# Row-maxima mask in four quarters of the array, routing in 18 steps, transposed maxima copied by ScalarE

## The chip, the cores and the metric

The kernel runs on one core of a Trainium2 chip. The metric is the device time of one execution in microseconds (us). An iteration below is one pass of the attention loop, in which one sequence of 512 rows goes through; there are 16 sequences.

## The reference, cut to what matters

```python
# x: (16, 512, 128); 16 heads of 8; 8 experts, hidden width 512; float32
x = _layernorm(x + attention(x))            # causal softmax attention
# mixture of experts on xn, which is x normalized once more, with gamma and beta
probs = softmax(xn @ Wg.T)                  # 8 experts
top1 = argmax(probs); top2 = argmax(probs without top1)
t1v, t2v = probs[top1], probs[top2]
gates = [t1v, t2v] / (t1v + t2v + 1e-9)
out = sum over the two of gate * (gelu(xn @ W1[e] + b1[e]) @ W2[e] + b2[e])
x = _layernorm(x + out)
```

With `best` the largest logit and d the second largest minus best, the gates are 1/z and exp(d)/z, z = 1 + exp(d) + 1e-9 * sum(exp(logit - best)).

## The kernel before, in words

Attention and routing run in one software pipeline, `iterations`: in iteration i the kernel computes the scores and values of sequence i, the row maxima of sequence i (second half) and of sequence i+1 (first half), the output projection of i-1, the gating input of i-2 and the routing of i-2 and i-3. An iteration has 16 steps h. The order of each engine is written out by hand, as a function `body` for each. The expert stage (lines 1129 to 1145) and the last normalization follow; neither is touched by the diff.

The maxima of a sequence are taken in 24 units (`maxima`, line 1011). In a unit TensorE multiplies queries by keys into one of three slots of `ring` (line 1037: stationary 64 rows by 128 columns, once for each half of the array's rows, so that two heads run beside each other), adds the causal mask by a product of a diagonal and `pastb` in bfloat16 (line 1052: four products a unit), and VectorE reduces the slot (`maximum`, line 1189). 16 of the 24 units mask one block of 128 columns in each head, 8 mask two. The scores (`scores`, line 1006) use the slots in turn with them: unit n of the scores waits for the maximum of unit n-2 to be taken, unit n of the maxima for the exponentials of scores unit n-1. The scores, the products of queries and keys and the mask all use the array as two tiles of 64 rows by 128 columns; the small products of line 973 and the projections (899, 904, 910, 934, 965) and transposes (888) use it whole, the values (1069) and the transposes of the maxima (917) in tiles of 128 by 32.

The maxima of a group of four heads and their rounding rest (`split_max`) are transposed by TensorE into `ps_m` (`st_mT`, line 917, at h = 1, 5, 9, 13), copied to `mt` (`copy_max`, line 1218, VectorE, right after the first maximum of that step) and placed beside the queries by a DMA on ScalarE's queue (`place_max`, at h = 2, 6, 10, 14). `ps_m` is used by one thing after another in the order of `MISC`: after mT come kT (h = 2, line 899), uT (h = 6 and 14) and nT (h = 10), and each waits for `freed` of the one before.

Routing is a list of 20 steps (`ROUTING`, line 1258), one or two small VectorE operations each, with a semaphore between one step and the next. Steps 0 to 5 of sequence i-2 stand at half-steps 26 to 31 of an iteration, 6 to 11 of i-3 at half-steps 0 to 5, the rest at 9 to 16. Lines 1283 to 1287 (steps 15 to 19) make the gates, at half-steps 12 to 16: half-step 14 is h = 7. In h = 6 and later GpSimd masks probabilities (line 598), writes rows by indirect DMA (line 610) and multiplies by gamma (line 664, h = 7).

## Time and profile before

| | |
|---|---|
| median of 3 runs | 1107.22 us (1107.21 to 1108.87) |
| profiled execution, its own time | 1104.55 us |
| its span | 1102.5 us |
| PE busy | 959.9 us, 87% |
| DVE (VectorE) busy | 816.1 us, 74% |
| ACT (ScalarE) busy | 665.9 us, 60% |
| POOL (GpSimd) busy | 637.5 us, 58% |
| granted TensorE clock, mean | 0.971 |
| chain that ended last | PE 50%, DVE 20%, issue 10%, DMA 6%, POOL 6% |

The busy shares are means over the whole span. The pipeline of attention and routing fills about two thirds of it, and the expert stage the rest. The chain that ended last is followed back from the last instruction, at each step to what released it. Ends of PE's products are modelled; their starts are what to compare.

### The profile page before, as it was taken

What the parts mean: (1) busy time and instruction counts of PE and PEld (TensorE: products, weight loads), DVE (VectorE), ACT (ScalarE), POOL (GpSimd) and SP (SyncE); (2) the same over time, 40 slices, a digit from 0 to 9 for tenths busy, and PEclk for the clock granted to TensorE, in tenths of its full rate; (3) what the DMA queues carried; (4) which work ended last, traced back from release to release, by engine and by line L of the source; (5) the groups of instructions that cost most, each with busy time, mean ns of one, the idle gap of its engine ahead of it and who ended that gap; (6) DMA issues with size and microseconds to landing.
All of it is one profiled execution on the core that took longest, in us unless ns stands there. A gap on an engine that the chain in (4) does not pass through costs nothing.

```text
span 1102.5 us, 29583 instructions
## 1 busy us (share of the span) xinstructions
PE 959.9 (87%) x9185; PEld 635.4 (58%) x9185; DVE 816.1 (74%) x2134; ACT 665.9 (60%) x1338; POOL 637.5 (58%) x951
## 2 busy tenths in 40 slices
PE   3789999999999999999999999869899889998750
PEld 1344454454545545545544455339899879998740
DVE  3777879888888888898898888954454464467744
ACT  1256566676666676666666766636566745556552
POOL 7022434754855756657647557547757556557874
PEclk9899999999999999999999999979999999999985
DMA  7523133243243242332432423343322222265515
GB/s 163 191 79 114 52 105 113 60 139 104 65 129 105 86 123 83 114 118 71 125 116 54 137 92 90 104 144 78 86 69 85 74 74 78 72 215 171 170 50 171
DMA packets 134567, 117.74 MB, mean 107 GB/s; under 512 B 56218, under 2 KB 99777, under 8 KB 134240
## 3 DMA queue, kind: packets, MB, share of 16 engines
q1 hardware_dynamic: 121808, 96.37, 30.0%
q0 software_dynamic: 8704, 17.06, 4.6%
q10 hardware_dynamic: 3904, 2.43, 1.0%
q8 instruction: 78, 1.28, 0.5%
q14 instruction: 73, 0.60, 0.2%
HBM read 65.26 MB, written 53.81 MB: 108 GB/s over the span
## 4 chain that ended last, share of the span: by engine, by line
PE 50%; DVE 20%; issue 10%; DMA 6%; POOL 6%; ACT 3%; SPq 3%; ACTq 1%; DVEq 0%; POOLq 0%
PE ring L1145 9%; PE ring L1129 9%; DVE negmax L1189 9%; PE ps_v L1069 7%; PE ring L1006 6%; PE ring L1037 5%; PE ring L1052 3%; SPq L397 2%; POOL y_d L633 2%; PE ps_m L899 2%; PE ps_m L917 2%; DVE rv L1285 2%; PE ps_m L934 2%; PE ps_m L904 1%; DVE mt L1218 1%
## 5 line engine op out<-in xcount | busy, mean ns | idle before, releaser
L728 ACT ACTIVATE probs<-ring 128x768 f32<-128x768 f32 (+1 forms) x384 | 337.5, 882 | 211.9 <-PE ring L1006 208.3
L1189 DVE TENSOR_REDUCE negmax<-ring 128x2 f32<-128x1024 f32 (+3 forms) x512 | 410.6, 815 | 62.7 <-PE ring L1052 56.3
L598 POOL TENSOR_SCALAR_AFFINE_SELECT probs<-probs 128x512 f32<-128x512 f32 x256 | 163.1, 639 | 287.0 <-ACT probs L728 285.4
L837 ACT ACTIVATE vpad<-ring,b_s 128x128 f32<-128x128 f32 x576 | 164.3, 369 | 104.9 <-PE ring L1129 103.7
L633 POOL DMA_INDIRECT y_d<-vpad,xs x144 | 146.6, 1018 | 109.9 <-DVE vpad L1488 80.5
L1006 PE MATMUL ring<-qarea,kside 64*128 64x512 f32 (+3 forms) x1024 | 177.7, 385 | 28.6 <-DVE negmax L1189 20.0
L1006 PEld LDWEIGHTS ring<-qarea,kside 64*128 64x128 f32 x1024 | 86.6, 185 | 183.1 <-issue 119.4
L1069 PE MATMUL ps_v<-probs,vpad 128*32 128x512 f32 (+3 forms) x2048 | 180.7, 449 | 4.0 <-POOL probs L598 4.0
L1037 PE MATMUL ring<-kside,qarea 64*128 64x256 f32 (+2 forms) x1024 | 165.0, 360 | 17.3 <-DMA qarea<-qk_d 10.4
L1145 PE MATMUL ring<-qarea,vpad 128*128 x1152 | 158.6, 281 | 18.3 <-ACT vpad L837 17.8
L1129 PE MATMUL ring<-vpad,w_t 128*128 128x128 f32 x1152 | 156.2, 279 | 8.9 <-issue 8.5
L1145 PEld LDWEIGHTS ring<-qarea,vpad 128*128 128x128 f32 x1152 | 140.6, 192 | 26.6 <-issue 23.9
L1129 PEld LDWEIGHTS ring<-vpad,w_t 128*128 128x128 f32 x1152 | 141.2, 193 | 13.3 <-issue 12.9
L610 POOL DMA_INDIRECT rows_d<-xn,slot x128 | 128.8, 1006 | 25.9 <-issue 24.4
L1052 PE MATMUL ring<-pastb,diagb 64*128 64x128 bf16 (+1 forms) x1536 | 125.4, 242 | 0.0
L1037 PEld LDWEIGHTS ring<-kside,qarea 64*128 64x128 f32 x1024 | 88.3, 189 | 30.6 <-issue 10.5
L1472 DVE COPY w_t<-kside 128x512 f32 x144 | 64.6, 449 | 54.1 <-PE ring L1129 42.2
L1488 DVE TENSOR_TENSOR vpad<-ring,xin 128x128 f32<-128x128 f32 x144 | 42.0, 291 | 83.1 <-PE ring L1145 77.9
L1052 PEld LDWEIGHTS ring<-pastb,diagb 64*128 64x128 bf16 x1536 | 45.1, 96 | 54.9 <-issue 39.9
L1069 PEld LDWEIGHTS ps_v<-probs,vpad 128*32 128x32 f32 x2048 | 44.9, 109 | 47.4 <-issue 36.3
L852 ACT ACTIVATE probs<-probs,zrs 128x128 f32<-128x128 f32 x64 | 27.5, 488 | 42.8 <-POOL zrs L697 42.8
L1515 DVE SCALAR_TENSOR_TENSOR probs<-probs,gates 128x128 f32<-128x128 f32 x128 | 35.9, 343 | 11.3 <-DMA probs<-x_d 11.2
(178 smaller groups left out, 1092.5 us busy)
## 6 DMA issues: line engine op xcount, KB each, us to landing
qk_d<-qarea SPq DMA_DIRECT2D x62, 256.0 KB, 2.5
kside<-qk_d SPq DMA_DIRECT2D x96, 128.0 KB, 3.0
qarea<-qk_d SPq DMA_DIRECT2D x90, 128.0 KB
xs<-rows_d SPq DMA_DIRECT2D x144, 66.0 KB, 1.9
probs<-y_d SPq DMA_DIRECT2D x16, 512.0 KB, 4.5
xin<-L_attn_x SPq DMA_DIRECT2D x16, 256.0 KB, 2.9
att_d<-attt SPq DMA_DIRECT2D x128, 32.0 KB
rows<-att_d SPq DMA_DIRECT2D x16, 256.0 KB
```

The lines of the kernel that those rows point to most:

```text
L598: pool.affine_select(out=diag, in_=diag, pattern=[[0, 4], [1, P]], compare_op=ALU.is_ge, fill=0.0, base=0, channel_multiplier=-1).then_inc ...
L610: pool.indirect_dma_start(rows_d, bass.IndirectOffsetOnAxis(ap=slot[:, late.parity, k, q:q + 1], axis=0), xn[:, late.parity, q, k, :], Non ...
L633: pool.indirect_dma_start(y_d, bass.IndirectOffsetOnAxis(ap=xs[:, n % RING, D:D + 1].bitcast(I32), axis=0), ys[:, n % RING, :], None, boun ...
L728: nc.scalar.activation(of_unit(h // 2, part), ring[:, 2 * part % 3, :, (0, P, P)[part]:S], ACT.Exp, scale=SCALE).then_inc(sem("exp_done"), 1)
L837: ins = nc.scalar.activation(ht[:, n % 4, c, :], ps_a[:, n % 4, c * P:(c + 1) * P], ACT.Gelu_apprx_tanh, bias=b1_s[:, bass.ds(e, 1), c:c + ...
L1006: ins = pe.matmul(ring[:, 2 * n % 3, half, c0:c0 + S - q0], kside[rows, i.parity, e, g, kb * P:(kb + 1) * P], qside[i.parity][rows, g, q0: ...
L1037: pe.matmul(ring[:, (2 * n + 1) % 3, half, c0:c0 + nk], qside[b.parity][rows, g, qb * P:(qb + 1) * P], kside[rows, b.parity, e, g, 0:nk], ...
L1052: ins = pe.matmul(to, diagb[rows, at:at + P], past, start=False, stop=(c == 1))
L1069: ins = pe.matmul(ps_v[32 * j:32 * j + 32, kb * P:S], vpad[:, b.parity, kb, h, :], of_block(h, kb), start=(g % 2 == 0 and kb == 0), stop=( ...
L1129: ins = pe.matmul(ps_a[:, n % 4, c * P:(c + 1) * P], w1_t[:, n % 2, c * P:(c + 1) * P], xst[:, n % 4, :], start=True, stop=True)
L1145: ins = pe.matmul(ps_s[:, n % 2, 0:D], ht[:, n % 4, c, :], w2_s[:, bass.ds(e, 1), c, :].rearrange("p a d -> p (a d)"), start=(c == 0), sto ...
L1189: ins = nc.vector.tensor_reduce(negmax[:, n // 6 % 2, qb, s:s + 2], ring[:, (2 * n + 1) % 3, :, c0:c0 + nk], AX.X, ALU.max, negate=True)
```

## The change

The mask of a unit is made by four products of 64 by 64 instead of four of 64 by 128: queries 0 to 63 of a block against its 128 keys, queries 64 to 127 against its last 64 keys only, each for both row halves. So the product is written to 64 partitions at a time, and the second pair streams 64 columns for 128 (in the 8 units with two blocks 256 and 128 columns, where it was 256 twice). Routing has 18 steps: the first equality is folded into the multiplication by the table, the difference to the second logit comes out of the reduction itself, and z is one reduction over ten terms, for which ScalarE's exponential has a bias of log(1e-9) and a term of 1 is set once. `copy_max` moves from VectorE to ScalarE, where it stands at the end of h = 1, 5, 9, 13.

```diff
-    ROUTE = 20
+    ROUTE = 18
-        diagb = sb("diagb", [P, 3 * P // 2], BF16)
+        diagb = sb("diagb", [P, P // 2], BF16)
+        terms = sb("terms", [P, QB, E + 2])
+        tiny = sb("tiny", [P, 1])
...
+            pool.memset(terms[:], 1.0)
+            pool.memset(tiny[:], math.log(1e-9))
...
+                        if u == 2 and h % 4 == 1:
+                            copy_max(act, *((i, 1), (i, 2), (i, 3), (nxt, 0))[h // 4])
...
+            def copy_max(act, b, g):
+                if not b.exists(NB):
+                    return
+                need(act, ready("mT"), 4, b, g + 1)
+                need(act, sem("max_placed"), 64, b, 16 * g)
+                nc.scalar.activation(mt[:], ps_m[0:2 * GH, :], ACT.Copy).then_inc(freed("mT"), 1)
...
-                        nc.scalar.activation(rt[:, 2], rt[:, 1], ACT.Exp).then_inc(sem("gate_exp"), 1)
+                        nc.scalar.activation(terms[:, :, 0:E], rt[:, 1], ACT.Exp, bias=tiny[:, :]).then_inc(
+                            sem("gate_exp"), 1)
-                    need(act, sem("route"), ROUTE, i.plus(-3), 8)
-                    nc.scalar.activation(rv[:, 4], rv[:, 3], ACT.Exp).then_inc(sem("gate_exp"), 1)
+                    need(act, sem("route"), ROUTE, i.plus(-3), 7)
+                    nc.scalar.activation(terms[:, :, E], rv[:, 3], ACT.Exp).then_inc(sem("gate_exp"), 1)
...
                 for c in range(2):
-                    at = HALF * (1 - c)
+                    queries = slice(HALF * c, HALF * (c + 1))
                     for half in range(2):
                         rows = half_of(half)
-                        to = ring[:, (2 * n + 1) % 3, half, :]
-                        past = pastb[rows, at:at + P]
+                        to = ring[queries, (2 * n + 1) % 3, half, :]
+                        past = pastb[rows, HALF:(3 - c) * HALF]
                         if n % 3 == 2:
-                            to = to.rearrange("p (a n) -> p a n", n=P)[:, 0:QB:QB - 1, :]
-                            past = past.unsqueeze(1).broadcast_to([HALF, 2, P])
+                            to = to.rearrange("p (a n) -> p a n", n=P)[:, 0:QB:QB - 1, c * HALF:P]
+                            past = past.unsqueeze(1).broadcast_to([HALF, 2, P - c * HALF])
                         else:
                             c1 = (QB - 1 - n % 3) * P
-                            to = to[:, c1:c1 + P]
-                        ins = pe.matmul(to, diagb[rows, at:at + P], past, start=False, stop=(c == 1))
+                            to = to[:, c1 + c * HALF:c1 + P]
+                        ins = pe.matmul(to, diagb[rows, :], past, start=False, stop=True)
...
-                lambda b: [V.tensor_tensor(eq1, lg[:], along(best, E), ALU.is_equal),
-                           V.tensor_tensor(diff, lg[:], along(best, E), ALU.subtract)],
-                lambda b: [V.tensor_tensor(w1c, eq1, wtab[:], ALU.mult)],
+                lambda b: [V.tensor_tensor(diff, lg[:], along(best, E), ALU.subtract)],
+                lambda b: [V.scalar_tensor_tensor(out=w1c, in0=diff, scalar=0.0, in1=wtab[:], op0=ALU.is_equal,
+                                                  op1=ALU.mult)],
...
-                lambda b: [V.tensor_reduce(v2, rest, AX.X, ALU.max)],
-                lambda b: [V.tensor_tensor(eq2, rest, along(v2, E), ALU.is_equal),
-                           V.tensor_tensor(d_best, v2, best, ALU.subtract)],
+                lambda b: [V.tensor_reduce(d_best, rest, AX.X, ALU.max)],
+                lambda b: [V.tensor_tensor(eq2, rest, along(d_best, E), ALU.is_equal)],
...
-                lambda b: [V.tensor_reduce(z, ex, AX.X, ALU.add)],
-                lambda b: [V.scalar_tensor_tensor(out=z, in0=z, scalar=1e-9, in1=e2, op0=ALU.mult, op1=ALU.add)],
-                lambda b: [V.tensor_scalar(z, z, 1.0, None, ALU.add)],
+                lambda b: [V.tensor_reduce(z, terms[:, :, :], AX.X, ALU.add)],
                 lambda b: [V.reciprocal(g(b, 0), z)],
                 lambda b: [V.tensor_tensor(g(b, 1), e2, g(b, 0), ALU.mult)],
...
-                        if h % 4 == 1 and not half:
-                            copy_max(gb, gg)
-                        if 12 <= at < 17:
+                        if 12 <= at < 15:
                             route(late, 3 + at)
```

VectorE's `copy_max` (line 1212) is gone. The product of line 1287 now stands at half-step 14, where the addition of line 1285 stood, and the reciprocal at half-step 13.

## Rows read from the trace of the kernel before

**Rows 1.** Windows: us, busy us and count per engine, TensorE clock, DMA share, GB/s.

```profile
44.40:728.20 683.80, 638.37 (x6533) 339.17 (x6533) 591.70 (x1294) 451.34 (x656) 383.70 (x584) 0.99 0.34 101
```

**Rows 2.** Line 1006: duration ns minimum/median/maximum, first and last start, us.

```profile
L1006 PE MATMUL ring<-qarea,kside x1024: 217/415/792, 44.4 to 728.2; 64*128 64x512 f32 x43, 64*128 64x128 f32 x43, 64*128 64x256 f32 x43, 64*128 64x384 f32 x42
```

**Rows 3.** Waits: engine, line, releaser; us in total, times, longest us.

```profile
PEld ring L1006 <- DVE negmax L1189: 50.9, 91, 1.1
...
PEld ps_m L899 <- DVE mt L1218: 5.6, 9, 0.7
```

**Rows 4.** Groups by line and form: busy us, mean ns; then idle us, releaser.

```profile
L1218 DVE COPY mt<-ps_m 8x512 f32<-8x512 f32 x64 | 42.8, 668 | 0.7 <-PE ps_m L917 0.7
...
L1285 DVE TENSOR_SCALAR rv<-rv 128x4 f32<-128x4 f32 x16 | 24.5, 1531 | 0.0
...
L1284 DVE SCALAR_TENSOR_TENSOR rv<-rv 128x4 f32<-128x4 f32 x16 | 4.0, 248 | 0.0
...
L1272 DVE TENSOR_TENSOR rv<-rv 128x4 f32<-128x4 f32 x16 | 6.7, 421 | 0.0
...
L1286 DVE RECIPROCAL gates<-rv 128x4 f32<-128x4 f32 x16 | 2.6, 163 | 0.0
...
L806 ACT ACTIVATE xnt<-ps_m 128x512 f32<-128x512 f32 x16 | 9.6, 600 | 1.0 <-PE ps_m L888 1.0
```

**Rows 5.** Timeline, PE alone: start us, us, engine, line, operation, tiles.

```profile
347.32 0.50 PE L1006 MATMUL ring<-qarea,kside 64*128 64x512 f32 x2
...
347.65 0.40 PE L1037 MATMUL ring<-kside,qarea 64*128 64x512 f32 x2
...
347.89 0.28 PE L1052 MATMUL ring<-pastb,diagb 64*128 64x128 bf16 x4
...
348.11 1.12 PE L899 MATMUL ps_m<-xt,wk_s 128*128 128x512 f32 x2
...
351.19 0.39 PE L1052 MATMUL ring<-pastb,diagb 64*128 64x256 bf16 x4
...
351.51 1.12 PE L904 MATMUL ps_m<-xt,wq_s 128*128 128x512 f32 x2
...
355.23 0.45 PE L1006 MATMUL ring<-qarea,kside 64*128 64x384 f32 x2
...
355.61 0.19 PE L973 MATMUL ring<-onehot,lowerb 128*128 128x40 bf16 x1
...
356.11 0.28 PE L1052 MATMUL ring<-pastb,diagb 64*128 64x128 bf16 x4
...
356.20 0.42 PE L1006 MATMUL ring<-qarea,kside 64*128 64x256 f32 x4
```

**Rows 6.** Timeline around the routing step of line 1285, one iteration.

```profile
448.14 1.11 POOL L610 DMA_INDIRECT rows_d<-xn,slot  x1 [0.17 <-issue]
...
449.22 1.97 DVE L1285 TENSOR_SCALAR rv<-rv 128x4 f32<-128x4 f32 x1
...
449.27 0.65 POOL L598 TENSOR_SCALAR_AFFINE_SELECT probs<-probs 128x512 f32<-128x512 f32 x1
...
449.87 1.29 POOL L664 TENSOR_TENSOR xc<-xc,gam_b 128x512 f32<-128x512 f32 x1
...
450.77 0.29 PE L1052 MATMUL ring<-pastb,diagb 64*128 64x128 bf16 x4
...
451.58 0.44 PE L1006 MATMUL ring<-qarea,kside 64*128 64x384 f32 x2 [0.52 <-DVE negmax L1189]
...
451.64 1.22 DVE L1189 TENSOR_REDUCE negmax<-ring 128x2 f32<-128x1024 f32 x1
...
452.91 0.44 PE L1006 MATMUL ring<-qarea,kside 64*128 64x256 f32 x4 [0.46 <-DVE negmax L1189]
```

**Rows 7.** Timeline, a two-input DVE operation beside a GpSimd DMA.

```profile
376.02 0.97 POOL L610 DMA_INDIRECT rows_d<-xn,slot  x1 [0.17 <-issue]
...
376.14 0.18 DVE L1209 TENSOR_TENSOR mhl<-negmax,mhl 128x16 fp32r<-128x16 f32 x1
```

More of the change, by code:

```diff
@@ L16 @@
 from contextlib import ExitStack
+import math
 import concourse.bass as bass
@@ L555, in _ @@
             link(pool.memset(lowerb[:], 0.0))
-            mid = diagb[:, HALF:2 * HALF]
-            link(pool.affine_select(out=mid, in_=mid, pattern=[[-1, HALF]], compare_op=ALU.not_equal, fill=1.0,
+            link(pool.affine_select(out=diagb[:], in_=diagb[:], pattern=[[-1, HALF]], compare_op=ALU.not_equal, fill=1.0,
                                     base=0, channel_multiplier=1))
-            pool.affine_select(out=mid, in_=mid, pattern=[[-1, HALF]], compare_op=ALU.not_equal, fill=1.0,
+            pool.affine_select(out=diagb[:], in_=diagb[:], pattern=[[-1, HALF]], compare_op=ALU.not_equal, fill=1.0,
                                base=-HALF, channel_multiplier=1)
@@ L1210, in split_max @@
                                             mhl_of(0).bitcast(F32), ALU.subtract).then_inc(sem("max_split"), 1)
-            def copy_max(b, g):
-                if not b.exists(NB):
-                    return
-                need(dve, ready("mT"), 4, b, g + 1)
-                need(dve, sem("max_placed"), 64, b, 16 * g)
-                nc.vector.tensor_copy(mt[:], ps_m[0:2 * GH, :]).then_inc(freed("mT"), 1)
             def low_part(b, side, name, high, stage):
@@ L1251, in _ @@
             V = nc.vector
-            best, d_best, z, e2, c1, v2, c2 = (rv[:, k] for k in (0, 3, 6, 4, 1, 2, 5))
-            eq1, diff, ex, w1c, m1, rest, eq2, w2c, m2, place, p1, p2 = (rt[:, k] for k in range(12))
+            best, d_best, z, c1, c2 = (rv[:, k] for k in (0, 3, 6, 1, 5))
+            diff, w1c, m1, rest, eq2, w2c, m2, place, p1, p2 = (rt[:, k] for k in (1, 3, 4, 5, 6, 7, 8, 9, 10, 11))
+            e2 = terms[:, :, E]
             def g(b, k):
@@ L1259, in _ @@
                 lambda b: [V.tensor_reduce(best, lg[:], AX.X, ALU.max)],
-                lambda b: [V.tensor_tensor(eq1, lg[:], along(best, E), ALU.is_equal),
-                           V.tensor_tensor(diff, lg[:], along(best, E), ALU.subtract)],
-                lambda b: [V.tensor_tensor(w1c, eq1, wtab[:], ALU.mult)],
+                lambda b: [V.tensor_tensor(diff, lg[:], along(best, E), ALU.subtract)],
+                lambda b: [V.scalar_tensor_tensor(out=w1c, in0=diff, scalar=0.0, in1=wtab[:], op0=ALU.is_equal,
+                                                  op1=ALU.mult)],
                 lambda b: [V.tensor_reduce(c1, w1c, AX.X, ALU.max)],
                 lambda b: [V.tensor_tensor(m1, wtab[:], along(c1, E), ALU.is_equal)],
-                lambda b: [V.scalar_tensor_tensor(out=rest, in0=m1, scalar=NEG, in1=lg[:], op0=ALU.mult,
+                lambda b: [V.scalar_tensor_tensor(out=rest, in0=m1, scalar=NEG, in1=diff, op0=ALU.mult,
                                                   op1=ALU.add)],
-                lambda b: [V.tensor_reduce(v2, rest, AX.X, ALU.max)],
-                lambda b: [V.tensor_tensor(eq2, rest, along(v2, E), ALU.is_equal),
-                           V.tensor_tensor(d_best, v2, best, ALU.subtract)],
+                lambda b: [V.tensor_reduce(d_best, rest, AX.X, ALU.max)],
+                lambda b: [V.tensor_tensor(eq2, rest, along(d_best, E), ALU.is_equal)],
                 lambda b: [V.tensor_tensor(w2c, eq2, wtab[:], ALU.mult)],
@@ L1306, in route @@
                 if n == 15:
-                    need(dve, sem("gate_exp"), 2, b, 1)
-                if n == 16:
                     need(dve, sem("gate_exp"), 2, b, 2)
```

## The prediction

> **What bounds the kernel now.** I read the windows first. From the first product of scores to the last (44.4 to 728.2 us) [rows 2] TensorE is busy for 638.4 of 683.8 us and VectorE for 591.7 [rows 1]. That is 16 iterations of 42.7 us, with TensorE idle for (683.8 - 638.4) / 16 = 2.8 us in each. So the attention stage is bound by TensorE, and VectorE stops it briefly. The expert stage, which the diff leaves alone, is not counted further. A faster VectorE alone can give back at most these 45 us. What TensorE waits for is in the waits: before the scores' weights 91 waits for a row maximum, 50.9 us, much of which lies under products still running; before kT 9 waits for the copy to `mt`, 5.6 us [rows 3]. The timeline of one iteration shows where the waits for maxima stand: at h = 8 (0.52 us) and at h = 9 (0.46 us), just behind a routing step of 1.97 us [rows 6].
>
> **What is taken from VectorE.** By the groups: the copies 42.8 us, line 1285 24.5, line 1284 4.0, line 1272 6.7 [rows 4], and a first equality of about 0.17 us (my estimate, from the reciprocal's 163 ns) for 16 sequences, 2.7. Sum 80.7 us, 5.0 us an iteration. Little of it is on the path, since TensorE has only 2.8 us of idleness to give. So each piece is priced by the wait that it causes:
>
> - Line 1285 takes 1.97 us for four numbers a row. It starts at 449.22, when an indirect DMA of GpSimd is ending (448.14 + 1.11 = 449.25), and is done at 451.19, as GpSimd's mask (449.27, 0.65 us) and gamma product (to 451.16) are [rows 6]. It is kept out by GpSimd. Behind it stand the next maxima: the one of 1.22 us starts at 451.64, and the scores at 452.91 wait for it. Its input, the mask at 450.77, was complete at 451.06. Without the step the maximum starts 0.56 us earlier, and then it is limited by its own mask. Of the two waits of 0.98 us, 0.56 goes.
> - At half-step 14 there now stands the gate product, with two operands in SBUF. Does it stall the same way? A two-operand step at 376.14 takes 0.18 us while an indirect DMA runs from 376.02 to 376.99 [rows 7], so the DMA doesn't hold it. It has to start before GpSimd's mask at 449.27. It would start at 449.22 less what the reciprocal saves against line 1284 (248 - 163 = 85 ns [rows 4]), about 449.13. I take it to pass, by a margin of 0.14 us.
> - The same 0.09 us bring the attention output, the transpose after it and what follows earlier.
> - The copies: TensorE's waits of 5.6 us before kT [rows 3] go, 0.35 us an iteration.
> - The second operation of step 7 (line 1272) takes 0.42 us on average for four numbers [rows 4]; it too is held up at times. Between 0 and 0.42 us of it reach TensorE; I take 0.20.
>
> Sum: 0.56 + 0.09 + 0.35 + 0.20 = 1.20 us an iteration.
>
> **What ScalarE takes on.** Four copies an iteration; no row has this shape, the nearest has 128 x 512 from PSUM: 600 ns [rows 4]. That is 2.4 us more on an engine busy for 451.3 of 683.8 us [rows 1]. The copy stands behind the exponentials of its step. Behind it on ScalarE are the exponentials of the next step, whose scores TensorE issues only after the transposes and values. In these units products, transposes and values lie between; cover of over 1 us, so I take nothing. If ScalarE were late by its whole length in each, the bound would be 2.4 us an iteration.
>
> **What the mask costs TensorE.** From starts in the timeline of TensorE [rows 5]: after queries by keys of 512 columns (347.65) the mask starts 0.24 us later. The mask of 128 columns gives way to scores in the same tiles after 0.09 us (356.11 to 356.20), but to the whole array (kT, qT) after 0.22 (347.89 to 348.11); the one of 256 columns after 0.32 (351.19 to 351.51). So 2 x 128 more columns cost 0.10, and a product in another tile shape starts 0.13 later. Coming in, the first scores after another shape take 0.33 us for 512 columns (347.32 to 347.65) against 0.24, so 0.09 more for weights that could not be loaded ahead. (Columns are reckoned at the 2.4 GHz level; the granted clock of the stretch is 0.99 of it [rows 1].) Before line 973, in another shape and with small weights, 384 columns take 0.38 us (355.23 to 355.61); 0.09 for those weights and 384 / 2400 = 0.16 leave 0.13, where within one shape 0.24 - 512 / 2400 = 0.03 is left: 0.10 more. The quarters (64 by 64) are another shape than the 64 by 128 before them. I take this 0.10 us at each of the 24 entries, and 0.13 + 0.09 = 0.22 at the exits where the next product had the mask's shape (h = 4 on the path; the others, at h = 8, 12 and 0, fall where TensorE has slack).
>
> Against it stand the columns: the four quarters can run beside each other. For 128 columns the group took 0.09 with four starts in it, near what four starts need, so I take a gain of 0.02 (bounds 0 and 0.05); for 256 columns 0.10 (bounds 0 and 0.16). So a unit of one block costs 0.08 more and one of two blocks nothing. Of the 24 units of an iteration 14 lie in stretches where TensorE never waits (9 of one block, 5 of two); of the other 10, one feeds the maximum at h = 8 and gives 0.10 back, and the rest is taken up by the idleness that stays (2.8 - 1.2 us). Sum: 9 x 0.08 + 0.22 + 0.10 = 1.04 us an iteration.
>
> The pause is the reading on which the sign turns. The Trainium skill, TensorEngine Tiling (Array Packing), Key Properties, says that a change of the tiling mode, not of the tile alone, drains TensorE; by that rule the entries pay, as I have charged them from the rows. The same page says that separate tiles work in parallel; by that alone, the mask would only gain.
>
> **The sum.** 1.20 - 1.04 = 0.16 us an iteration, 2.6 us in 16, and about 0.6 for one copy and shorter maxima while the pipeline fills (estimate, one copy of 0.67 [rows 4]). The profiled execution's own time, 1104.55 us, becomes 1101.4; it stands 2.7 us under the median of the runs, which so becomes 1104.
>
> **Rivals.**
>
> *No pause (0.27).* Quarters behind halves follow without a pause, as one 64-row tile follows another. For it: all four lie in the same two row halves. Against it: each change of shape in rows 5 has one, the one from 128 x 128 to line 973's neighbours too. Then TensorE gains 9 x 0.02 + 5 x 0.10 = 0.68, VectorE's 1.20 stays, nothing is charged: 1.9 us an iteration, 30 us: 1077.
>
> *The stall only changes hands (0.16).* If the gate product comes 0.14 us later against GpSimd than I reckon (a longer mask in h = 6 could do it), it is locked out for the same 1.9 us, and the 0.56 and 0.10 of h = 8 are lost, less 0.16 for the reciprocal that no longer follows: 0.40 us an iteration, 6.4 us: 1110, slower than before. For it: the place and GpSimd's work are the same, and both read SBUF. Against it: rows 7. The point is the start of GpSimd's mask at h = 7.
> The Trainium skill, SBUF — State Buffer, Who interferes with whom, has it that a VectorE operation with two SBUF inputs contends with a GpSimd one that reads SBUF, and that the order of issue decides.
>
> *The pause is dearer (0.12).* With 0.13 us at each entry, as at the exits, and no gain from the columns of one block: 9 x 0.13 + 5 x 0.03 + 0.22 + 0.13 = 1.67, and the exits at h = 12 and 0 with the six units around them outrun the slack by some 0.4: 2.07 - 1.20 = 0.87 us, 14 us: 1121. For it: the entries behind 348.11 and 351.51 show 0.13. Against it: line 973's 0.10 [rows 5].
>
> *ScalarE is late (0.05).* At h = 5 it also copies v and normalizes; if uT waits 0.4 us for the freed bank there, 6.4 us: 1110.
>
> **Chances and range.** The forecast has 0.40: half of it is faster by over 0.2% (2.2 us, about what can be told from no change here), 0.11 within, 0.09 slower. No pause is faster (0.27). The stall: 0.04 same, 0.12 slower. The dearer pause: slower. ScalarE: 0.01 same, 0.04 slower. Faster 0.20 + 0.27 = 0.47, same 0.16, slower 0.37. The forecast's own range is 1095 to 1114 (0.6 us an iteration to either side). The whole range is 1074 to 1118: the lower end takes in most of the case without a pause, the upper one the stall and a part of the dearer pause.
>
> **What would show it.** In the changed profile, line by line: the queries-by-keys products to the mask, start to start, 0.34 us for 512 columns if there is a pause, 0.24 if not; the mask of 256 columns to qT 0.22 and not 0.32; the gate product at h = 7 at 0.16 us if it passes, near 1.9 if not; the wait at h = 8 gone and the one at h = 9 under 0.2 us; no wait of kT on the copy; VectorE busy for some 735 us. The prediction is wrong if the entries show no pause, if the gate product stalls, or if an iteration takes under 41.5 or over 43.5 us.

## The result, and the profile after

The changed kernel takes 1116.77 us (median of six runs, 1112.53 to 1119.31) where the kernel before takes 1108.05 on the same chip (six runs, 1106.90 to 1111.04). The ratio is 1.0069, with a 95% interval of 1.0042 to 1.0096. Forecast was 1104, a little faster; it is slower by 8.7 us. The profiled execution took 1117.87 us, 13.3 more than that of before.

The page, first the engines and then the chain that ended last:

```profile
span 1116.1 us, 29505 instructions
PE 989.1 (89%) x9185; PEld 642.5 (58%) x9185; DVE 779.9 (70%) x2006; ACT 700.0 (63%) x1402; POOL 635.4 (57%) x953
...
PE 69%; DVE 8%; issue 7%; DMA 5%; ACT 4%; POOL 4%; SPq 2%; ACTq 1%; POOLq 0%; DVEq 0%
```

VectorE is busy for 36 us less and stands on the chain with 8% where it had 20%. TensorE is busy for 29 us more with the same number of instructions. So the bound did not move to a new engine: TensorE, which already set the pace, got slower.

The window from the first product of scores to the last, as in [rows 1], with the same columns:

```profile
42.60:735.90 693.30, 663.33 (x6533) 342.39 (x6533) 556.35 (x1178) 485.33 (x719) 381.73 (x584) 0.98 0.33 99
```

The stage takes 693.3 us for 683.8, of which TensorE is idle for 30.0 where it was 45.4 (length less PE busy). To part slower work from slower clock I cut the stage into windows of 2 us and summed (1 - granted clock) x 2 us: 5.5 us before, 17.1 after. What is left as work (length less idle less this) is 632.9 before and 646.2 after. So the 9.5 us of the stage are 13.3 of work more, 15.4 of idleness less and 11.6 of clock lost. (The sum counts the lost clock in full, also where TensorE would have waited anyway, so it is an upper estimate of what the clock took.) The other 4 us of the two profiled executions lie mostly in the expert stage (326.0 us for 321.4).

Waits, as [rows 3]:

```profile
PEld ring L1023 <- DVE negmax L1208: 31.1, 41, 1.4
...
PE ring L1023 <- DVE negmax L1208: 14.4, 26, 1.0
```

The weights of the scores wait 41 times for a maximum where it was 91 times, and no row of kT on the copy is left. The groups of [rows 4], line 1285 and the copy (columns as there; the second row is ScalarE's):

```profile
L1297 DVE TENSOR_TENSOR gates<-terms,gates 128x4 f32<-128x4 f32 x16 | 25.7, 1604 | 0.0
...
L797 ACT ACTIVATE mt<-ps_m 8x512 f32<-8x512 f32 x64 | 37.0, 578 | 23.3 <-PE ps_m L934 23.0
```

The sum of z is one step now and costs 0.18 us, but the gate product, which now stands where line 1285 stood, costs what line 1285 did (24.5 us in all) [rows 4].

The timeline of TensorE, as [rows 5] (keys products are line 1054 now, the mask 1071):

```profile
351.81 0.45 PE L1054 MATMUL ring<-kside,qarea 64*128 64x256 f32 x4
352.19 0.30 PE L1071 MATMUL ring<-pastb,diagb 64*64 64x256 bf16 x4
352.41 1.13 PE L921 MATMUL ps_m<-xt,wq_s 128*128 128x512 f32 x2
...
354.59 0.40 PE L1054 MATMUL ring<-kside,qarea 64*128 64x512 f32 x2
354.92 0.24 PE L1071 MATMUL ring<-pastb,diagb 64*64 64x128 bf16 x4
355.09 1.16 PE L927 MATMUL ps_m<-wv_s,xt 128*128 128x128 f32 x8
...
357.14 0.24 PE L1071 MATMUL ring<-pastb,diagb 64*64 64x128 bf16 x4
357.31 0.45 PE L1023 MATMUL ring<-qarea,kside 64*128 64x256 f32 x4
357.60 0.46 PE L1054 MATMUL ring<-kside,qarea 64*128 64x256 f32 x4
```

and, in the kernel before, the keys products that follow the last row of [rows 5]:

```profile
356.59 0.50 PE L1037 MATMUL ring<-kside,qarea 64*128 64x256 f32 x4
```

Start to start: keys products of 512 columns to the mask 0.33 us (0.24 before), a mask of one block to the whole array 0.17 (0.22), of two blocks 0.22 (0.32), and back to the scores' shape at h = 4 0.17 (0.09). The pause is there, and going in it has the size that was charged. Coming out, the 0.08 us are made up at once: the keys products follow the scores after 0.29 us where it was 0.39, so from the mask to them it is 0.46 us (0.48).

The timeline of three engines around the old stall, as [rows 6]:

```profile
363.33 1.11 POOL L616 DMA_INDIRECT rows_d<-xn,slot  x1 [0.17 <-issue]
...
363.70 0.69 DVE L1208 TENSOR_REDUCE negmax<-ring 128x2 f32<-128x512 f32 x1
...
364.31 2.07 DVE L1297 TENSOR_TENSOR gates<-terms,gates 128x4 f32<-128x4 f32 x1
364.46 0.65 POOL L604 TENSOR_SCALAR_AFFINE_SELECT probs<-probs 128x512 f32<-128x512 f32 x1
...
365.06 1.28 POOL L670 TENSOR_TENSOR xc<-xc,gam_b 128x512 f32<-128x512 f32 x1
...
366.76 0.44 PE L1023 MATMUL ring<-qarea,kside 64*128 64x384 f32 x2 [0.59 <-DVE negmax L1208]
...
368.10 0.44 PE L1023 MATMUL ring<-qarea,kside 64*128 64x256 f32 x4 [0.54 <-DVE negmax L1208]
...
369.73 1.94 PE L1088 MATMUL ps_v<-probs,vpad 128*32 128x512 f32 x8
```

The product of four numbers a row takes 2.07 us, to the end of GpSimd's gamma product (366.34). The two waits for maxima are both still there, 0.59 and 0.54 us for 0.52 and 0.46. And then something that no step of mine had: the values at 369.73 take 1.94 us, while the same eight products took 1.06 eleven us earlier. Windows around it, with the columns of [rows 1]; the clock is the one before the last two:

```profile
364.00:366.00 2.00, 2.00 (x28) 1.06 (x28) 2.00 (x2) 1.23 (x2) 1.98 (x3) 1.00 0.12 39
366.00:368.40 2.40, 1.27 (x18) 0.82 (x18) 2.37 (x6) 2.04 (x3) 1.61 (x3) 1.00 0.27 58
368.40:369.30 0.90, 0.90 (x15) 0.61 (x12) 0.79 (x2) 0.76 (x3) 0.81 (x3) 0.96 0.42 66
369.40:372.70 3.30, 3.30 (x14) 0.70 (x12) 0.73 (x2) 1.22 (x3) 2.92 (x5) 0.51 0.29 54
```

TensorE was busy for 1.27 of the 2.4 us of the two waits; a microsecond later it is granted 0.51, the level of 1.2 GHz, for 3.3 us, though it is busy throughout. This comes back in nine iterations, each time in h = 8 to 10 (324.6, 368.6, 412.6, 456.6, 500.6, 546.6, 590.6, 634.6, 678.6). A tenth fall, at 730.6, stands at the end of the stage, where the kernel before has one too (720.4). The waits alone don't bring it: two earlier iterations in the same profile have the same two, 0.59 and 0.54 us, and no fall, as this one:

```profile
235.68:238.08 2.40, 1.27 (x18) 0.82 (x18) 2.37 (x6) 2.05 (x3) 1.62 (x3) 1.00 0.27 59
238.80:242.40 3.60, 3.60 (x36) 1.67 (x36) 2.25 (x3) 2.77 (x6) 3.22 (x5) 1.00 0.30 59
```

In the profile of before the place shows the same two waits and no fall (the iteration of [rows 6]):

```profile
450.90:453.30 2.40, 1.43 (x20) 0.88 (x16) 2.40 (x8) 2.12 (x3) 1.61 (x3) 1.00 0.31 64
453.30:457.00 3.70, 3.70 (x37) 1.73 (x36) 2.95 (x5) 2.31 (x4) 3.23 (x6) 1.00 0.29 48
```

### The profile page after: what moved, and what is told of

It is laid out like the page before. It is cut to its first block, busy times and chain, and to the rows that moved or that the text cites. A ratio compares the mean times of both kernels' runs of the same rounds, so it can differ in the third digit from the quotient of the medians.

```text
span 1116.1 us, 29505 instructions
## 1 busy us (share of the span) xinstructions
PE 989.1 (89%) x9185; PEld 642.5 (58%) x9185; DVE 779.9 (70%) x2006; ACT 700.0 (63%) x1402; POOL 635.4 (57%) x953
## 3 DMA queue, kind: packets, MB, share of 16 engines
q8 instruction: 78, 1.28, 0.5%
## 4 chain that ended last, share of the span: by engine, by line
PE 69%; DVE 8%; issue 7%; DMA 5%; ACT 4%; POOL 4%; SPq 2%; ACTq 1%; POOLq 0%; DVEq 0%
PE ps_v L1088 12%; PE ring L1023 10%; PE ring L1164 10%; PE ring L1148 9%; PE ring L1054 8%; PE ring L1071 4%; PE ps_m L934 3%; PE ps_m L905 3%; DVE negmax L1208 2%; DVE gates L1297 2%; ACT probs L734 2%; PE ps_m L916 2%; PE ps_m L951 2%; PE ps_m L921 2%; POOL y_d L639 1%
## 5 line engine op out<-in xcount | busy, mean ns | idle before, releaser
L1023 PE MATMUL ring<-qarea,kside 64*128 64x512 f32 (+3 forms) x1024 | 180.4, 390 | 17.7 <-DVE negmax L1208 14.4
L1088 PE MATMUL ps_v<-probs,vpad 128*32 128x512 f32 (+3 forms) x2048 | 187.5, 463 | 4.5 <-POOL probs L604 4.5
L1164 PE MATMUL ring<-qarea,vpad 128*128 x1152 | 158.7, 281 | 19.2 <-ACT vpad L854 19.2
L616 POOL DMA_INDIRECT rows_d<-xn,slot x128 | 128.8, 1006 | 25.8 <-issue 24.3
L1071 PE MATMUL ring<-pastb,diagb 64*64 64x128 bf16 (+2 forms) x1536 | 102.1, 244 | 0.0
L1071 PEld LDWEIGHTS ring<-pastb,diagb 64*64 64x64 bf16 x1536 | 43.8, 104 | 91.9 <-issue 75.7
L797 ACT ACTIVATE mt<-ps_m 8x512 f32<-8x512 f32 x64 | 37.0, 578 | 23.3 <-PE ps_m L934 23.0
```

What stands on the lines that cost most here:

```text
L616: pool.indirect_dma_start(rows_d, bass.IndirectOffsetOnAxis(ap=slot[:, late.parity, k, q:q + 1], axis=0), xn[:, late.parity, q, k, :], Non ...
L1023: ins = pe.matmul(ring[:, 2 * n % 3, half, c0:c0 + S - q0], kside[rows, i.parity, e, g, kb * P:(kb + 1) * P], qside[i.parity][rows, g, q0: ...
L1071: ins = pe.matmul(to, diagb[rows, :], past, start=False, stop=True)
L1088: ins = pe.matmul(ps_v[32 * j:32 * j + 32, kb * P:S], vpad[:, b.parity, kb, h, :], of_block(h, kb), start=(g % 2 == 0 and kb == 0), stop=( ...
L1164: ins = pe.matmul(ps_s[:, n % 2, 0:D], ht[:, n % 4, c, :], w2_s[:, bass.ds(e, 1), c, :].rearrange("p a d -> p (a d)"), start=(c == 0), sto ...
```

## The experiments

Every kernel was timed in five rounds against the kernel before on the same chip. There are two sorts of chips: on some the kernel before takes 1108 to 1109 us, on others 1137 to 1143, almost all of it in the expert stage (some 359 us for 321). So I compare ratios, and in profiles the attention stage alone. The kernel before has a profile of the first sort only.

Theories. A: the pause at the changes of shape cancels the gains of the routing and the copy. B: the stall only changed hands. C, which came from the profile after: the waits that stay, together with the new shape, bring the clock down. The letters are not used alike in all the expectations. In the first four, B is that the clock falls only because of the waits behind the stall, and A takes in that the quarters lower it by themselves. In those of `after_again` and `short_late` C is the quarters' or the fewer columns' effect on the clock, and in that of `filled` the waits'. The first four give times for a chip of the first sort; they were run on one of the second, where only the ratios can be compared with them.

**One part at a time, and the stall.** The first four ran on one chip, of the second sort.

`mask_only`: the kernel before with the quarters alone (the hunk of `maxima` and `diagb`).

> The kernel before with the mask in quarters and nothing else. Theory A (the quarters cost: a pause at each change of tile shape, and less work in the array, so that TensorE's clock is granted at 1.2 GHz in places): 1118 to 1128 us, granted clock of the attention stage at 0.98 or below, since VectorE's relief is missing. Theory B (the clock falls only because of the wait behind the stalled gate product, the quarters cost 0.03 us a unit): 1108 to 1114 us, and since the old stall of 1.97 us is there too, the clock may fall or not.

`rest_only`: the changed kernel with the mask of before, so the copy and the routing alone.

> The changed kernel with the old mask in halves: routing in 18 steps and the copies on ScalarE. Theory A: 1092 to 1101 us, clock of the attention stage 1.00 as before. Theory B: the gate product still stalls for about 2.0 us at h = 7, the clock falls behind it as in the changed kernel, 1105 to 1112 us.

`product_late`: the changed kernel with the gate product two half-steps later, past GpSimd's mask and gamma product:

```diff
-                        if 12 <= at < 15:
-                            route(late, 3 + at)
+                        if at in (12, 13, 16):
+                            route(late, min(3 + at, 17))
```

> The changed kernel with the gate product (routing step 17) at half-step 16, behind h = 7. Both theories: the product takes 0.16 us and the waits of 0.59 and 0.54 us at h = 8 and 9 become less than half. Theory A (quarters take down the clock by themselves): the clock still falls, 1106 to 1112 us. Theory B (the clock falls behind the waits at h = 8 and 9): the clock stays at 1.00 and the time is 1092 to 1100 us.

`rest_late`: the same edit in `rest_only`.

> Old mask in halves, routing in 18 steps with the gate product at half-step 16, copies on ScalarE. If the stalled product costs 0.56 us an iteration or more, this is 6 to 12 us faster than the same kernel with the product at half-step 14: Theory A 1084 to 1092 us, Theory B 1090 to 1098 us. Against the kernel that has the quarters and the late product it gives the price of the quarters without a stall: 8 to 16 us by theory A, 0 to 5 us by theory B.

Measured, ratio to before:

| | ratio | interval |
|---|---|---|
| `mask_only` | 1.0013 | 0.9995 to 1.0031 |
| `rest_only` | 0.9904 | 0.9877 to 0.9930 |
| `product_late` | 0.9974 | 0.9954 to 0.9994 |
| `rest_late` | 0.9884 | 0.9854 to 0.9915 |

Copy and routing bring 1%, the quarters alone cost next to nothing, and yet the two together are slower than before. The mask costs 0.1% by itself, 0.9% beside the rest with the late product (0.9974 against 0.9884), and with the stall 1.5% (1.0051 in the second run of the changed kernel, on a chip of the same sort, against 0.9904). The late product does what it should; its source row (ns, minimum/median/maximum), the changed kernel first and then `product_late`:

```profile
L1297 DVE TENSOR_TENSOR gates<-terms,gates x16: 153/2066/2069, 191.4 to 906.4; 128x4 f32<-128x4 f32 x16
```

```profile
L1297 DVE TENSOR_TENSOR gates<-terms,gates x16: 146/153/737, 197.6 to 928.6; 128x4 f32<-128x4 f32 x16
```

and what is left of the scores' waits in `product_late` is

```profile
PE ring L1023 <- DVE negmax L1208: 1.1, 2, 0.6
```

14.4 us in 26 waits became 1.1 in 2. So the stall was only handed on, and without it the changed kernel is 0.8% better, and just faster than before. But what it gives is not the wait's time. TensorE is idle for 28.5 us of the stage where it was 30.0: waits for exponentials (11.1 us where they were 7.0) and for the rows of the attention output (7.4, were 1.3) stand in the place of those for maxima. Less the lost clock, by the windows of 2 us, the stage takes 677.3 us with the late product and 676.2 with the stall. What differs over all runs is the clock, 0.9685 against 0.9614 in `after_again`, 12 runs each: 0.0071 of 1145 us is 8 us (my estimate), nearly all of the 0.8%. With the mask in halves the late product does shorten the stage by itself (666.1 us for 672.0 less the lost clock, `rest_late` and `rest_only`), but the ratios differ by 0.2% only.

Of the expectations, at the ratios to 1108 us: `mask_only` (1109.4) came out as B had it and `rest_only` (1097.4) as A had it, though the stall of 2.07 us that B foresaw is there. `product_late` (1105.1) lies between both, with the waits gone, as both had it, and falls of the clock left, against B. `rest_late` (1095.1) is in B's range, but only 2 us under `rest_only`, for 6 to 12, and the quarters cost 10 us beside it, which is A's 8 to 16.

**The changed kernel again, and columns without the shape.** All four on one chip of the second sort.

`after_again` is the changed kernel.

> The changed kernel once more, on the chip of the other experiments. Theory A (the quarters cost by the pause, 4 to 11 us of the attention stage once the rest no longer hides it; the stalled gate product costs another 6; together they eat what routing and copies give): ratio to the kernel before 0.999 to 1.005. Theory C (the quarters also take the granted clock down, which the kernel before escapes): 1.005 to 1.010, with the clock of its runs at least 0.003 under that of the kernel before in the same call.

`short_late`: `rest_late`, its mask in halves of 64 by 128, but the second product over the last 64 columns only, as the quarters have it:

```diff
                 for c in range(2):
                     at = HALF * (1 - c)
+                    k0 = HALF * c
...
-                        past = pastb[rows, at:at + P]
+                        past = pastb[rows, at + k0:at + P]
...
-                            to = ...[:, 0:QB:QB - 1, :]
-                            past = past.unsqueeze(1).broadcast_to([HALF, 2, P])
+                            to = ...[:, 0:QB:QB - 1, k0:P]
+                            past = past.unsqueeze(1).broadcast_to([HALF, 2, P - k0])
...
-                            to = to[:, c1:c1 + P]
+                            to = to[:, c1 + k0:c1 + P]
```

> Routing in 18 steps with the gate product at half-step 16, copies on ScalarE, and the mask in the old halves of 64 by 128, its second product over the last 64 columns of a block only (128 of 256 where there are two blocks): the quarters' columns without their shape. If the shape is what costs (theory A), no pause is seen and the time is 2 to 6 us under the kernel with the same rest and the full halves: ratio 0.980 to 0.986. If it is the fewer columns that let the clock fall (theory C in its other form), ratio 0.990 to 1.000 with more falls of the clock.

`short_only`: the same edit in the kernel before.

> The kernel before with the second mask product over half of its columns, in the old halves. Nothing else changed. Theory A: TensorE gives back 0.02 us for one block and 0.05 for two, where it isn't waiting for VectorE: 0 to 4 us, ratio 0.996 to 1.000. Theory C: slower, 1.001 to 1.006, by the clock.

`shape_only`: the kernel before with quarters in which both products cover all 128 columns, so the shape without the saved columns.

> The kernel before with the mask in quarters of 64 by 64 and all columns of before in each product: the shape without the fewer columns. Theory A: the pause of 0.09 us at each entry and the exits stay, and the columns lie beside each other as far as the four quarters work in parallel: a group of one block 0.01 to 0.03 us shorter than in halves, of two blocks 0.10 shorter, so nearly the time of the quarters alone, ratio 1.001 to 1.006. If the quarters did not work beside each other, their groups would be as long as in halves and the ratio 1.008 or more.

Measured: `after_again` 1.0051 (1.0025 to 1.0078), `short_late` 0.9853 (0.9819 to 0.9886), `short_only` 0.9989 (0.9963 to 1.0014), `shape_only` 1.0009 (0.9985 to 1.0033). `after_again` came out as C had it (clock 0.006 under before), `short_late` and `short_only` as A, and `shape_only` at the edge of A's range. The pause belongs to the shape: with all the columns kept, the timeline of TensorE in `shape_only` has the mask 0.32 us behind its keys products, and the next shape 0.18 behind it.

```profile
302.56 0.40 PE L1036 MATMUL ring<-kside,qarea 64*128 64x512 f32 x2
302.88 0.25 PE L1052 MATMUL ring<-pastb,diagb 64*64 64x128 bf16 x4
303.06 0.66 PE L887 MATMUL ps_m<-ident,xin 128*128 128x128 f32 x4
```

`short_late` is the best version, 1.5% under the kernel before (1122.93 us for 1141.32): the copy, the short routing, the late gate product, and the saved columns in the old shape. Its window:

```profile
42.40:708.50 666.10, 631.24 (x6533) 342.57 (x6533) 549.25 (x1174) 481.98 (x719) 384.04 (x584) 0.99 0.35 103
```

TensorE is busy for 631.2 us, 7 less than in the kernel before and 32 less than in the changed one.

**The clock, and each half of the rest.** All three on one chip of the first sort.

`filled`: the changed kernel with one product of zeros by ones more before each of the two waiting scores. It adds zero to the values' bank; nothing else is changed, the stall least of all.

```diff
+            def fill(i):
+                if i.exists(NB):
+                    pe.matmul(ps_v[:], none[:], some[:], start=False, stop=False, skip_group_check=True)
...
+                    if h == 9:
+                        fill(i)
                     scores(i, h // 2, 2 if h % 2 else 0)
...
+                    if h == 8:
+                        fill(i)
                     if h % 2 == 0:
                         scores(i, h // 2, 1)
```

> The changed kernel with one product of zeros by 512 columns (it adds nothing to the accumulated values) ahead of the scores that wait at h = 8 and one ahead of those at h = 9, 32 in all, where TensorE waits 0.59 and 0.54 us for row maxima; each takes 0.21 us of streaming and up to 0.3 with its change of tile. Theory C (the waits behind the stalled gate product are what takes the clock down to 1.2 GHz in the changed kernel): mean granted clock of its runs 0.966 or more, against 0.961 of the changed kernel, and the ratio 0.998 to 1.003 in place of 1.005. Theory A (the clock has nothing to do with these waits; only pauses and stalls count): clock 0.961 as before, ratio 1.005 to 1.012.

`copy_only`: the kernel before with `copy_max` on ScalarE.

> The kernel before with the copies of the transposed maxima on ScalarE and nothing else. By the prediction (0.35 us an iteration, the wait of kT) 5.6 us: ratio 0.993 to 0.997. If VectorE's relief of 0.67 us at each of four places counts wherever row maxima are late, 8 to 12 us: 0.989 to 0.993. If ScalarE is late with it: 1.000 or more.

`routing_only`: the kernel before with the routing of 18 steps.

> The kernel before with the routing in 18 steps, the gate product at half-step 14 as in the changed kernel, and nothing else. The stall of 2.0 us stands where it stood, so it gives little: the time of the reciprocal and of four short steps, 0 to 4 us, ratio 0.996 to 1.000. If the short steps that GpSimd holds up were what mattered: 0.990 to 0.995.

Measured: `filled` 0.9978 (0.9961 to 0.9996), `copy_only` 0.9917 (0.9900 to 0.9934), `routing_only` 0.9937 (0.9917 to 0.9958). `filled` came out as C had it, or a trace better, `copy_only` and `routing_only` in the ranges of their second cases, better than the prediction's terms. More work on the engine that is the bound makes the kernel faster. The stall is untouched:

```profile
L1309 DVE TENSOR_TENSOR gates<-terms,gates x16: 152/2062/2070, 191.3 to 888.9; 128x4 f32<-128x4 f32 x16
```

but the clock does not fall behind it. The windows of `filled` at the place of those shown above, and the whole stage:

```profile
364.90:367.30 2.40, 1.89 (x23) 1.25 (x22) 2.37 (x6) 1.93 (x3) 1.62 (x3) 1.00 0.34 68
368.30:371.60 3.30, 3.30 (x33) 1.58 (x36) 1.85 (x4) 2.47 (x5) 2.92 (x5) 1.00 0.31 60
...
42.70:721.80 679.10, 653.71 (x6547) 343.05 (x6565) 555.32 (x1167) 484.90 (x719) 381.78 (x583) 1.00 0.35 101
```

No window of the stage shows a fall. The stage takes 14.2 us less than in the changed kernel; its lost clock went from 17.1 us to 0. This profile is of the fastest of its 12 runs (1100.35 us, clock 0.977; median 1105.69); by the ratios the changed kernel gains 0.7 to 0.9%, some 8 to 10 us. (The trace has 32 weight loads of the zero products and 16 records of the products themselves, so its TensorE busy time is a little short; the length is not.)

The mean granted clock of all runs, not of one profile: 0.9614 in 12 runs of `after_again` against 0.9674 in 29 of the kernel before beside it, 0.9685 in `product_late`, and 0.9753 in `filled` (0.973 to 0.977) against 0.9711 in 17 of the kernel before. Among the six runs of the changed kernel's first timing the one at 0.968 took 1112.53 us and the profiled one at 0.961 1117.87. One profile is a poor witness here: those of before, of `short_only` and of `rest_only` show 2, 2 and 1 falls, `mask_only` 9, `shape_only` 4, `product_late` 4, `rest_late` 7.

The length of an iteration (first product of scores to the next one's) parts the falls from the rest. Medians of the 12 iterations from the fourth on, those with a fall and those without, from one profile each:

| | without a fall, us | with a fall, us |
|---|---|---|
| before | 43.35 (12) | none |
| `copy_only`, `routing_only` | 42.47 (12 each) | none |
| `rest_only` | 42.46 (12) | none |
| `mask_only` | 42.93 (5) | 44.43 (7) |
| changed | 42.94 (3) | 44.45 (9) |
| `filled` | 42.94 (12) | none |
| `product_late` | 42.96 (10) | 46.48 (2, with longer falls) |
| `short_late` | 41.71 (10) | 44.87 (2) |

A fall costs the changed kernel 1.5 us. The zero products cost nothing that can be seen here, and neither the stall nor the late product changes an iteration without a fall while the mask is in quarters.

`short_filled`: `short_late` with a zero product at h = 8, between scores and maxima, where a wait of some 0.5 us was left.

> The fastest version so far (routing in 18 steps with the gate product at half-step 16, copies on ScalarE, mask in the old halves with the second product over half the columns) with one product of zeros by 512 columns at h = 8, between the scores and the maxima that wait about 0.5 us there for an exponential: 16 in all. If the clock is what that kernel still loses (6.8 us in its attention stage), its granted clock rises to 0.973 or more and the ratio falls to 0.978 to 0.984. If the product costs more than the clock gives: 0.985 to 0.989, against 0.985 without it.

0.9888 (0.9852 to 0.9923), against 0.9853: no gain. The clock of its runs is 0.9683 for 0.9692. This was the second case of its expectation, that the product costs more than the clock gives. A zero product helped where the falls are regular; here it was no improvement.

## Why the prediction was wrong

The forecast was that 1.20 us an iteration gained and 1.04 charged leave 2.6 us. Against the median that was measured, 1104 is off by 12.8 us. Two steps failed: the gate product was taken to pass, and the granted clock was taken to stay as it was, a term put at nothing without a reason. The second is where the time went.

**The pause and the columns: right, and at the entries in size too.** Charged for quarters: 0.10 at an entry (0.09 measured, 0.24 to 0.33), 0.22 at the exit of h = 4, 0.10 back for two blocks (0.10 measured). Two terms were off. The gain of one block behind which the array is used whole is 0.05, the upper bound, where I took 0.02. And the exit costs nothing there: 0.08 us to the scores, but the mask to the keys products takes 0.46 us for 0.48, and in the median of all such places (28 before, 31 after) 0.46 for 0.42. The rule of the Trainium skill, TensorEngine Tiling (Array Packing), Key Properties, that a change of mode drains the array, agrees with this trace at the entries; `shape_only` shows that it is the shape and not the columns. All in all TensorE has 13.3 us more work by the windows, where I had 1.04 x 16 = 16.6. "No pause" (1077) is refuted, and so is "the pause is dearer" (1121), whose 0.13 no entry shows. Nor is the work all loss: an iteration in quarters without a fall is 0.5 us longer than one in halves with the same rest (42.94 for 42.46), half of the 1.04.

**The stall of 0.56 us: this step failed.** I let the gate product pass "by a margin of 0.14 us", 449.13 against GpSimd's mask at 449.27. In the profile after the starts shown are 364.31 and 364.46: the very margin, and it takes 2.07 us in 12 of 16 iterations. The maximum ahead of it is shown to last to 364.39, 0.08 us past the product's start, so a start shown on VectorE doesn't tell exactly from when an operation works. That alone is not the reason, for in `product_late` the overlap and the margin are the same, and the product passes:

```profile
371.56 1.01 POOL L616 DMA_INDIRECT rows_d<-xn,slot  x1 [0.17 <-issue]
...
372.57 0.15 DVE L1297 TENSOR_TENSOR gates<-terms,gates 128x4 f32<-128x4 f32 x1
...
372.72 0.63 POOL L604 TENSOR_SCALAR_AFFINE_SELECT probs<-probs 128x512 f32<-128x512 f32 x1
```

What differs is the indirect DMA ahead. There it is over when the product starts (371.56 + 1.01 = 372.57); in the changed kernel it lasts to 364.44, 0.13 us past the start shown, and the mask follows 0.02 us behind it. Where it lasts longer and the mask comes later, in the changed kernel's first such iteration, the product ends just behind the DMA (191.77 and 191.70) and not 2 us later:

```profile
190.47 1.23 POOL L616 DMA_INDIRECT rows_d<-xn,slot  x1 [0.26 <-issue]
...
191.37 0.40 DVE L1297 TENSOR_TENSOR gates<-terms,gates 128x4 f32<-128x4 f32 x1
...
191.72 0.65 POOL L604 TENSOR_SCALAR_AFFINE_SELECT probs<-probs 128x512 f32<-128x512 f32 x1
```

So the premise that failed is most likely "so the DMA doesn't hold it". It rested on one operation near the start of a DMA [rows 7]; this one comes near the end of one. No run moves the DMA alone, so this is read from traces, not shown by an experiment. It was rival 2 as to what stalls, at a chance of 0.16, though not by the longer mask that I gave as the way to it. Its price was 0.40 us an iteration, so 1110; its own terms make 0.56 + 0.10 - 0.16 = 0.50, so 1112. The runs show neither: `product_late` has a median of 153 ns and waits of 1.1 us for 14.4, but its iterations without a fall are no shorter. The stall mattered through the clock behind its waits. The Trainium skill, SBUF — State Buffer, Who interferes with whom, has the contention and that the order of issue decides. The trace agrees on the contention: the held operation ends with GpSimd's mask (0.65 us) and product (1.28). On the order it doesn't bear the page out as it stands, for the product is shown to start 0.15 us before the mask and is held all the same.

**What none of my cases had: the clock.** Between the forecast and 1116.8 stand the clock's falls. By the windows of 2 us the attention stage without them would be 676.2 us against 678.3, 2.1 us shorter than before; `filled`, which had none, has 679.1 against the 683.8 of before, 4.7 shorter. The forecast had 2.6. So without the clock the sum would have come out near the mark, with the stall in it, and that is luck: the idleness fell by 15.4 and not 19.2 us, the work rose by 13.3 and not 16.6, and the stall that I took away stayed. What turned it to slower is the clock: 11.6 us more lost than before by the windows, nine falls at 1.5 us by the iterations. Shown by `filled`: the stall and every instruction left in place, the waits filled, no falls, and 1.0069 (1.0051 on the other chip) became 0.9978. The iterations without a fall have the same length in both kernels (42.94 us), so it isn't another pace of the loop that keeps the clock up.

I had read the granted clock in rows 1 (0.99) and used it only to justify reckoning at 2.4 GHz. What I should have asked is which waits stand close together, and what the products between them do. The Trainium skill, TensorE: Matmul & The Clock Gate, Part 1: The HAM clock gate, ties the clock to how busy TensorE has been of late; the trace agrees in that the falls stand behind waits, in a stage in which the engine is busy for 95.7% of the time, but two iterations with the same waits have none.

**Why the parts do not add.** Quarters alone 1.0013, copy and routing alone 0.9904, product 0.9917, measured 1.0051. The iterations show two reasons. The first is a gain that can be had once. In 8 of the 12 iterations the kernel before waits twice early on, for a maximum and for kT:

```profile
430.13 0.45 PE L1006 MATMUL ring<-qarea,kside 64*128 64x256 f32 x4 [0.59 <-DVE negmax L1189]
...
433.92 1.12 PE L899 MATMUL ps_m<-xt,wk_s 128*128 128x512 f32 x2 [0.50 <-DVE mt L1218]
```

Three of the four iterations without these waits take 42.45 to 42.49 us, and those with them 43.3 to 44.1. The copy alone, the routing alone and the quarters alone each remove both waits, so together they gain the 0.9 us no more than once. The second is the falls. `rest_only` has the stall (153/2070/2075 ns) and halves, and 1 fall, at the end of the stage; the changed kernel's two profiles, with quarters, show 10 and 12. `mask_only` has the stall of before and the quarters, and the falls too, behind waits of 0.46 and 0.42 us, shorter than the 0.52 and 0.46 behind which the kernel before has none. Its profile is of its slowest run, though, and over all its runs the clock is 0.9663 for 0.9680 and the time 0.1% longer. By the clock over all runs the falls come often where quarters and the long waits meet: 0.9614 in `after_again`, against 0.9685 without the stall and 0.9682 with halves. Why the quarters should do it is not shown. TensorE is busy for 1.27 of the 2.4 us of the two waits, where the halves had 1.43, but the same 1.27 stand where no fall follows (the rows at 235.68), and in `mask_only` it is busy for 1.52 of 2.4 us (238.06 to 240.46) ahead of a fall. `rest_late`, with halves, has 7 falls and a low clock (0.9645) with a good time, which this leaves open.

**The copy: right in kind, larger than reckoned.** ScalarE takes 572 ns for it (569 to 587), near the 600 ns of the row that I took as nearest, and "ScalarE is late" did not happen: who waits for it are aT's weights, once, 1.8 us. Priced at 0.35 us x 16 + 0.6 = 6.2 us; alone it gives 9.7 (1109.0 to 1099.27; by the interval of the ratio 7.3 to 11.1). Beside kT's waits those for maxima shrink, from 20.0 us in 42 to

```profile
PE ring L1016 <- DVE negmax L1199: 11.5, 23, 0.9
```

in `copy_only`. I had counted VectorE's 0.67 us before the next maximum as free but for kT; it wasn't. The early waits for a maximum (0.59 us) go with those of kT (0.50), 0.9 us in 8 of 12 iterations.

**The routing** gives 0.6% alone (7.3 us) although the stall stays in full. 0.20 + 0.09 us an iteration, 4.6 us, is what the forecast leaves it without the 0.56. The other 2.7 us fit the same two early waits, which are gone in `routing_only` too. Together the copy and the routing give 1.0%, less than their sum of 1.5%: they take from the same idleness.

**VectorE** is busy for 779.9 us, not 735: 80.7 us were taken off, 25.7 less the 2.6 of a free product came back with the stall. Of the other 21 us some 10 are my count: each operation that another follows at once is shown overlapping it by 0.08 us, so taking 128 of them off saves that much less than their durations (estimate). The rest are mostly operations held up in other places, as line 1293 at 359.21, in h = 5: 0.73 us for two operations.

## What to carry to other kernels

Where an operation stands in a slot in which the one before it was held up, expect it to be held too, look at every GpSimd instruction around it, the indirect DMAs with the rest, and move it to the other side of that work before taking the gain. And ask what takes a wait's place once it is gone: here it was other waits. Save columns within the tile shape that the neighbours have: the halves with a short second product got the quarters' columns without their pauses, and were the only new mask that cost nothing beside the rest (0.9853 with it, 0.9884 without, with intervals that overlap). And where TensorE is the bound, look for short waits that stand close together and at the granted clock right behind them in windows of 2 us: here two waits cost 0.5 us each and the clock behind them 1.5 more, in nine iterations of 16.

## What the runs showed of the hardware

- TensorE's granted clock can drop to the 1.2 GHz level for 3.3 us inside a stage in which the engine is busy for 95.7% of the time, and in a stretch without a gap: behind two waits of 0.59 and 0.54 us with 0.8 us of products between them (366.76 to 368.10 less 0.54). It does so in nine iterations and not in two others with the same waits. With a 0.39 us product of zeros in each wait it never did in the 679 us of the one stage profiled, and the mean clock of 12 runs was 0.9753.
- A VectorE operation on 128 x 4 numbers took 2.07 us as GpSimd's mask and multiplication ran behind one another, 153 ns a slot later in the same loop. It was held over both, though it is shown to start 0.15 us before the first; an indirect DMA of GpSimd was then still running.
- An indirect DMA of GpSimd can go together with a held VectorE operation by itself: the same product took 0.40 us, to the end of a DMA of 1.23 us (191.37), and a cast of 128 x 16 at 245.22 took 0.68 us, to 245.90, beside a DMA from 244.89 to 245.86, where others took 0.18.
- A change from tiles of 64 x 128 to tiles of 64 x 64, the row tile unchanged, costs 0.09 us going in. Coming out it costs 0.08 to the first product, of which the median place keeps 0.04 at the products after.
- Two sorts of chips run the same kernel in 1108 and in 1141 us; the attention stage is nearly alike on both (693.3 and 696.9 us for the changed kernel), and the expert stage of all kernels takes 321 to 326 on the one and 357 to 363 on the other.
